# Layer-0 gates of batch 0 computed head by head, own staging tiles for batch 0's keys and queries, and the last step's key-wise sums placed ahead of its outputs

## What is computed

```python
xn = _layernorm(x)
x = x + attn(xn) + ffn(xn)      # both read xn
# attn: 16 heads of 8 features, softmax attention over keys and values shared by all heads
#       q = (xn Wq^T + bq) * 8**-0.5 ;  k, v = split(xn Wkv^T + bkv)
# ffn ("SwitchHead"): 8 heads, 8 experts each, and per head a full 1024 x 1024 attention
def _get_sel_gate(x, w, route_scale):
    raw = einsum('bsd,ed->bse', x, w).reshape(B, S, H, E)        # 8 heads x 8 experts
    vals, idx = top_k(sigmoid(raw), 2)
    vals = vals / clip(vals.sum(-1, keepdims=True), 1e-09) * route_scale
    return (one_hot(idx, E) * vals[..., None]).sum(-2)           # a dense gate
v   = einsum('bshep,bshe->bhsp', xv, gate_v)       # values of a head: 8 experts, gated
att = softmax(einsum('bhqp,bhkp->bhqk', q, k) * SCALE)
out = einsum('bshep,hepd->bsd', ctx * gate_o, o_w)
```

## Time and profile before

| | us |
|---|---|
| median of 3 runs (lowest, highest) | 3180.81 (3178.78, 3181.18) |
| the profiled execution, its own time | 3167.05 |
| its span, from the first to the last instruction | 3165.2 |
| PE busy | 2945.3 (93%) |
| DVE busy | 2427.8 (77%) |
| POOL busy | 1846.8 (58%) |
| ACT busy | 1619.2 (51%) |
| the step loop's first matmul (L293) starts at | 55.16 |
| the last batch's projection (L444) starts at | 2572.41 |

### The profile page before, as it was taken

How to read it: one execution, slowest core, us unless ns; L and a number is a source line. 1 busy time by engine, 2 the same in 40 slices (tenths; PEclk the granted TensorE clock), 3 DMA queues, 4 the chain that set the end, 5 groups by cost and what they waited for, 6 DMA issues and landing times. The chain is left out here.

```text
span 3165.2 us, 51840 instructions
## 1 busy us (share of the span) xinstructions
PE 2945.3 (93%) x17486; PEld 2054.4 (65%) x17486; DVE 2427.8 (77%) x4551; ACT 1619.2 (51%) x3277; POOL 1846.8 (58%) x2277
## 2 busy tenths in 40 slices
PE   4999999999999999999999999999999965798997
PEld 2666666666676666666666666666676643466674
DVE  7788898888889988898898988888888652245343
ACT  1455555555555555555555555555555621444634
POOL 2556666666676666666666676666666535334330
PEclk7999999999999999999999999999999978899998
DMA  5000001100100110101001100010010021133222
GB/s 168 21 22 22 22 22 32 32 22 23 37 27 22 32 32 22 29 23 36 29 22 32 32 22 23 22 43 28 22 39 22 10 43 45 56 89 110 84 76 85
DMA packets 139849, 124.63 MB, mean 39 GB/s; under 512 B 28410, under 2 KB 122116, under 8 KB 139492
## 3 DMA queue, kind: packets, MB, share of 16 engines
q1 hardware_dynamic: 125892, 88.46, 10.0%
q0 software_dynamic: 10160, 30.17, 3.0%
q10 hardware_dynamic: 3536, 2.69, 0.5%
HBM read 97.49 MB, written 29.30 MB: 40 GB/s over the span
## 5 line engine op out<-in xcount | busy, mean ns | idle before, releaser
L849 POOL TENSOR_TENSOR m_vprod<-m_vprod 128x512 f32<-128x512 f32 x256 | 336.1, 1313 | 721.4 <-DVE m_vprod L1223 721.4
L1210 DVE TENSOR_REDUCE m_peaks<-m_ring 128x1 f32<-128x512 f32 x1024 | 643.4, 682 | 23.9 <-PE m_ring L293 22.7
L957 ACT ACTIVATE m_expA<-m_ring 128x512 f32<-128x512 f32 x1024 | 543.9, 605 | 162.4 <-PE m_ring L366 159.2
L928 ACT ACTIVATE m_prob<-m_ring,m_negs 128x512 f32<-128x512 f32 x512 | 347.4, 684 | 404.4 <-DVE m_negs L1261 403.6
L344 PE MATMUL m_ring<-m_probT,m_vs 128*128 128x256 f32 x2048 | 473.8, 384 | 11.7 <-DVE m_oprod L1294 10.2
L344 PEld LDWEIGHTS m_ring<-m_probT,m_vs 128*128 128x128 f32 x2048 | 379.9, 190 | 83.8 <-issue 35.1
L1294 DVE TENSOR_TENSOR m_oprod<-m_ring,m_go 128x512 f32<-128x512 f32 x512 | 347.4, 685 | 73.5 <-POOL k_x L862 44.8
L1223 DVE TENSOR_TENSOR m_vprod<-m_ring,m_gate 128x512 f32<-128x512 f32 x512 | 348.8, 685 | 68.2 <-PE m_ring L99 41.0
L1251 DVE TENSOR_REDUCE m_negs<-m_ring 128x1 f32<-128x512 f32 x512 | 346.0, 685 | 39.2 <-PE m_ring L99 37.0
L858 POOL TENSOR_TENSOR m_oprod<-m_oprod 128x512 f32<-128x512 f32 x256 | 327.9, 1281 | 70.6 <-DVE m_oprod L1294 70.4
L938 ACT ACTIVATE m_probT<-m_ring 128x512 f32<-128x512 f32 x512 | 301.0, 605 | 103.9 <-PE m_ring L332 98.3
(11 more groups left out here) (311 smaller groups left out, 5396.9 us busy)
## 6 DMA issues: line engine op xcount, KB each, us to landing
m_wraw<-in_v_w SPq DMA_DIRECT2D x32, 512.0 KB, 4.0
m_qf<-q_dram SPq DMA_DIRECT2D x128, 128.0 KB, 2.7
m_wraw<-in_o_w SPq DMA_DIRECT2D x32, 512.0 KB, 4.0
q_dram<-m_kf SPq DMA_DIRECT2D x24, 256.0 KB, 3.0
listed<-in_pad SPq DMA_DIRECT2D x6, 897.0 KB, 12.2
m_xg<-listed SPq DMA_DIRECT2D x39, 138.0 KB
m_rows<-answers SPq DMA_DIRECT2D x8, 512.0 KB, 4.0
sums_dram<-m_sumsT ACTq DMA_DIRECT2D x128, 18.0 KB
```

What stands on the lines that cost most here:

```text
L849: vchain(pool.tensor_tensor(vprod[:, 0:512], vprod[:, 0:512], vprod[:, 512:1024], ALU.add))
L928: act.activation(prob[t % 2][:, c * 512:(c + 1) * 512], ring.home["scores", n, t, c][:, :], ACT.Exp, bias=neg[t % 2], accum_out=den[n % 2] ...
L957: act.activation(expA[hh][:, c * 512:(c + 1) * 512], ring.home["scT", n, k, hh, c][:, :], ACT.Exp)\
L1210: v.tensor_reduce(peaks[:, t, hh, c:c + 1], ring.home["peaks", n, t, hh, c][:, :], AX.X, ALU.max)\
```

## The change

It has two parts. The first is at the start:

- batch 0's keys and queries get four staging tiles of their own, cut out of `m_probT` (`first_kf`); ACT doesn't wait any more between the halves, and its first copy into `m_probT` waits for the stores instead;
- PE makes batch 0's keys and queries ahead of its logits, ACT copies them ahead of the exponentials of the gates, and the upper half of x and of the first value weights comes behind these; the square root at the start isn't held by the wait for the constants any more;
- batch 0's gates are computed for one head at a time (`first_gates(h, part)`, over 128x128: 8 token tiles, 2 gates, 8 experts), in staging tiles cut out of `m_oT`. Head 0's 17 parts come ahead of the step loop, head h's in iteration i = h - 3, two parts at each place of `batch_work`, three at place 7.

```diff
+        h_v, h_one, h_c, h_other = (oT[:, k * P:(k + 1) * P].rearrange("p (g e) -> p g e", e=ES) for k in range(4))
+        first_kf = probT[0][:, :, :].rearrange("p t q -> p (t q)").rearrange("p (w q d) -> p w q d", w=2, q=2)
...
+        def kf_of(b, what, q):
+            return kf[:, :] if b else first_kf[:, what, q, :]
...
-                    if b or q:
+                    if b:
                         act.wait_ge(ks_ready, 2 * b + q)
-                        act.wait_ge(q_stored, 64 + (96 * b if b else 48 * q))
+                        act.wait_ge(q_stored, 64 + 96 * b)
...
+                def first_gates(h, part):
+                    if not 0 <= h < HS:
+                        return
+                    flat = gate_of[0][:, :, :].rearrange("p t (k g e) -> p (t k) g e", k=2, e=ES)[:, :, h, :]
+                    if part == 0:
+                        v.wait_ge(gates_exp, 4)
+                    gate_part(gs, part, flat, (h_v, h_one, h_c, h_other, h_m, h_pair, h_inv), 2 * TPB)
+                    if part == 16:
+                        gates_kept(v.tensor_tensor(flat, h_one, h_other, ALU.add))
...
                 def batch_work(i, place):
+                    for part in range(2 * place, 2 * place + 2 + place // 7):
+                        first_gates(i + 3, part)
...
+                lower_keys(0, 0)
+                lower_keys(0, 1)
                 for l in range(4):
                     keep_v32(0, l)
-                lower_keys(0, 0)
                 for part in range(17):
-                    gates(0, part)
-                lower_keys(0, 1)
+                    first_gates(0, part)
                 lower_qk()
-                for part in range(17, 34):
-                    gates(0, part)
                 for i in range(-2, N0 + 3):
+                    if i == N0 - 1:
+                        invert_dens(B - 1)
```

`gate_part` holds the 17 parts as they were, with the tiles as arguments. The second part of the change is at the end: the last step (n = 31) is taken out of the loop on PE and ACT and written out, with all its `scores_by_key`, `exps` and `sum_by_key` moved up between the rest, ACT's store of the sums behind them, and `invert_dens(B - 1)` on DVE ahead of its iteration 31:

```diff
+                keyed(last, 7)
+                outputs(last, 1, 0)
+                outputs(last, 1, 1)
+                turn(last, 4, 1)
+                sum_by_key(last, 7)
+                turn(last, 5, 0)
+                outputs(last, 2, 0)
...
+                key_exps(last, 7)
+                keep_turned(last, 4, 1)
+                keep_sums(last)
+                store_sums(last)
```

More of the change, by code:

```diff
@@ L368, in scores_by_key, with keyed @@
                         .then_inc(scT_made, 1)
+                def keyed(n, k):
+                    for hh in range(2):
+                        for c in range(2):
+                            scores_by_key(n, k, hh, c)
                 def sum_by_key(n, k):
@@ L483, in _ @@
                 turn_xn(0, 1)
-                for l in range(4):
-                    logits(0, l)
                 for q in range(2):
@@ L488, in _ @@
                     queries(0, q)
+                for l in range(4):
+                    logits(0, l)
                 qk_products()
-                for i in range(-2, N0 + 3):
+                for i in range(-2, N0):
                     outputs(i - 2, 7, 1)
@@ L638, in _ @@
                     values(i + 1, 3, 0)
+                last = N0 - 1
+                outputs(last - 1, 7, 1)
+                sum_by_key(last, 2)
+                keyed(last, 3)
+                weigh(last, 0)
+                sum_by_key(last, 3)
+                keyed(last, 4)
+                turn(last, 3, 0)
+                turn(last, 3, 1)
+                outputs(last, 0, 0)
+                outputs(last, 0, 1)
+                sum_by_key(last, 4)
+                keyed(last, 5)
+                scores(last, 4, 0)
+                scores(last, 4, 1)
+                weigh(last, 1)
+                sum_by_key(last, 5)
+                keyed(last, 6)
+                turn(last, 4, 0)
+                scores(last, 5, 0)
+                scores(last, 5, 1)
+                sum_by_key(last, 6)
+                keyed(last, 7)
[5 more added lines that the diff above has]
+                outputs(last, 2, 0)
+                turn(last, 5, 1)
+                scores(last, 6, 0)
+                outputs(last, 2, 1)
+                scores(last, 6, 1)
+                outputs(last, 3, 0)
+                weigh(last, 2)
+                turn(last, 6, 0)
+                scores(last, 7, 0)
+                scores(last, 7, 1)
+                outputs(last, 3, 1)
+                outputs(last, 4, 0)
+                turn(last, 6, 1)
+                outputs(last, 4, 1)
+                turn(last, 7, 0)
+                turn(last, 7, 1)
+                weigh(last, 3)
+                for t in (5, 6, 7):
+                    outputs(last, t, 0)
+                    outputs(last, t, 1)
+                turn_xo(B - 2, 0)
+                turn_xo(B - 2, 1)
                 routing(B - 2)
@@ L668, in store_queries @@
                         rows = slice(2 + part * HD, 2 + (part + 1) * HD)
-                        sp.dma_start(q_dram[b % 2][:, rows, q * 512:(q + 1) * 512], kf[:, :]).then_inc(q_stored, 16)
+                        sp.dma_start(q_dram[b % 2][:, rows, q * 512:(q + 1) * 512], kf_of(b, 1, q)).then_inc(q_stored, 16)
                 def load_queries(n):
@@ L958, in exps, with key_exps @@
                         .then_inc(exps_made, 1)
+                def key_exps(n, k):
+                    for hh in range(2):
+                        for c in range(2):
+                            exps(n, k, hh, c)
                 def keep_sums(n):
@@ L1045, in keep_queries @@
                     act.wait_ge(q_made, 2 * b + q + 1)
-                    act.wait_ge(ks_ready, 2 * (b + 1) if b else q + 1)
-                    if b or q:
+                    if b:
+                        act.wait_ge(ks_ready, 2 * (b + 1))
                         act.wait_ge(q_stored, 64 + 48 * (2 * b + q))
-                    act.activation(kf[:, :], ring.home["queries", b, q][:, :], ACT.Identity, bias=bq[:, :], scale=HD ** -0.5)\
+                    act.activation(kf_of(b, 1, q), ring.home["queries", b, q][:, :], ACT.Identity, bias=bq[:, :], scale=HD ** -0.5)\
                         .then_inc(q_kept, 1)
@@ L1089, in batch_work @@
                         routing_exps(early)
+                roots(1, slice(0, TPB))
                 act.wait_ge(consts_loaded, 16 * n_consts)
-                roots(1, slice(0, TPB))
                 keep_xnT(0, 0)
                 keep_xnT(0, 1)
-                upper_x(0)
-                upper_wv(0, ahead=True)
-                for l in range(4):
-                    sigmoid_exps(0, l)
                 for q in range(2):
@@ L1101, in _ @@
                     keep_queries(0, q)
+                for l in range(4):
+                    sigmoid_exps(0, l)
+                upper_x(0)
+                upper_wv(0, ahead=True)
                 keep_qk()
-                for i in range(-2, N0 + 3):
+                for i in range(-2, N0 - 1):
                     softmax(i, 2, 1)
@@ L1381, in gates @@
-                    if part == 6:
-                        gs(v.scalar_tensor_tensor(out=g_v[:, :, :], in0=g_one[:, :, :], scalar=3.0e38, in1=g_v[:, :, :],
-                                                  op0=ALU.mult, op1=ALU.add))
-                    if part == 7:
-                        gs(v.tensor_reduce(g_pair[:, 1, :], g_v[:, :, :], AX.X, ALU.min))
-                    if part == 8:
-                        gs(v.tensor_tensor(g_c[:, :, :], g_v[:, :, :], spread(g_pair[:, 1, :], ES), ALU.is_equal))
@@ L1679, in _ @@
                     gate_outputs(i + 1, 3, 1)
-                invert_dens(B - 1)
                 keep_routing(B - 2)
```

128 lines of the change are left out of this document (93 added, 35 removed).

## The result

The changed kernel took 3195.85 us (median of 5 runs, 3190.92 to 3203.52) against 3178.78 us of the kernel before in the same comparison (5 runs, 3165.74 to 3181.18): ratio 1.0071, 95% interval 1.0053 to 1.0089. (The quotient of the two medians is smaller, 1.0054; all ratios in this text are those of the timed comparison.) The forecast was 3160.8 us, the range 3151 to 3178. The profiled execution of the changed kernel took 3190.92 us with a span of 3189.1; that of before 3167.05 with 3165.2.

A forecast was written before the change was run, and what follows sets the result against it. PE was taken to bound the steps, with DVE close behind and its gates holding the start. Start -22.5, steps +10 and end -7.5 make -20 us: 3180.8 to 3160.8 us, range 3151 to 3178.

The forecast's parts named there:

- The start: Ahead of the step loop: PE's first matmul 22.5 us sooner, ends 18 and 23.5.
- The price in the steps: Step loop: moved gates cost 9 us of DVE a head and lengthen the steps by 10 us, ends 3 and 24.
- the two ends I had put: Steps' price: 3 us if gates nearly all fill idle time, 24 us if 4 us idle stay at 9 us a head.
- The rival "slower": Steps: POOL-DVE lock makes each two-input operation wait 0.6 us, 14.2 us a head, 51 us price, 3202 us; chance 0.07.
- The lock: Steps: DVE instructions with two SBUF inputs and GpSimd instructions reading SBUF lock each other out for a whole instruction.
- The decision point: Steps: the rival "slower" decides from a price of 30 us on, about 11 us for a head.
- The end: Layer 0's last outputs to its projection: PE starts the projection sooner, 7.5 us gained, ends 4 and 10.

The follow-up runs named there:

- `e_no_later`: The changed kernel with the gates of heads 1 to 7 of batch 0 left out; ratio to the kernel before 0.9919.
- The doses: The kernel before with DVE work added in every second iteration from 8 to 28: reductions lengthened 23 stretches by 64.4 us, two-input operations by 104.9 (traces only).
- `e_places`: The changed kernel with each later head's gate operations unchanged but moved to places 3, 4 and 6; ratio to the kernel before 1.0027.
- `e_reduce`: The changed kernel with nine 128x128 two-input operations of each of heads 1 to 7 replaced by reductions at the same places; ratio to the kernel before 1.0009.

## Why the prediction was wrong

- **The start** was right in kind and 3 us too large: 19.45 us for PE's entry, and 20.0 us where nothing is added behind it (`e_no_later`), in the range of 18 to 23.5. Both of its ways were later than I had them. The queries landed at 33.6, not 29.8, since the stores took 5.94 us instead of 3.6 and began a microsecond later. DVE was ready for the split at 32.7, not 30.4: head 0's gates began 1.7 us sooner than I had put, but took 10.6 us instead of 6.4, since I had charged nothing for POOL's start-up work beside them.
- **The price in the steps** is the step that failed: "the end where DVE's overrun is its busy time plus 1 us of idle time that stays, against the old length", 10 us, measured 51. DVE's work was sized rightly, 9 us a head against 9.1 measured (63.7 / 7), though not the way I had it: a few parts were held by up to 1.1 us each, not all by 0.2. What was wrong is that 7 to 9 us of its idle time would be used. The idle time stayed, 6.2 to 9.2 us in a stretch. These are short waits for products and sums of others, spread through the step. My reading of them is that work put in front of an instruction delays what PE and ACT need next, PE stops, and DVE then waits for PE. The waits bear it out: PE's grew from 2.4 to 17.7 us, 13.9 of them for DVE, and DVE's for PE from 11.8 to 15.7. Neither of the two ends I had put (3 and 24 us, with 4 us idle that stay) held it.
- I had drawn the slack from two stretches: 7 us more DVE (62.4 to 69.6) cost PE 0.2 us. That work is the next batch's gates, and it stands there in both. The doses show that more behind it is paid for: a stretch with 63.4 us of DVE became 5.2 us longer for 6.1 us of work put at one place. What makes the two differ (what stands beside the other batch's parts, or the order of PE's work around them) these runs don't settle.
- **The rival "slower"** had the figure, 51 us and 3202, and its mechanism in part. That it had the figure is luck. It took 14.2 us a head with 3 us idle that stay; measured were 9.1 us with 6 to 9, and the two errors cancel. The lock makes 16 to 20 of the 51 us (`e_places`, `e_reduce`), the amount of work 31 to 35. The decision point, 30 us, was about right: with 31 and 35 us the kernels are at 1.0009 and 1.0027.
- **What of it is PE's clock**: in the five long stretches PE's busy time grew by 20 us of the 41, at granted clocks of 0.92 to 1.00 against 0.96 to 1.00. One minus the granted clock, times the length, gives 3.4 us lost before and 16.4 now, so by this estimate the clock makes 13 of the 20; the other 7, 1.8 of them in a stretch at full clock, stay open. The clock fell in the stretches in which PE's idle time had grown, in the doses' too (0.98 and 0.94, PE busy 2.1 and 3.3 us more), but not in the fifth, where PE was idle for 5.5 us. No run held the clock up with the same waits, so how long the steps would be at full clock stays open.
- **The end** was right as a sum: 7.5 predicted, 7.9 in the trace, 7.3 timed. Within it two errors cancel, which is luck: `keep_routing` came 3.2 us sooner, not 1.3, and DVE's chain from there to the projection took 10.05 us, not 8.1, since POOL's work held its choice. PE idles 10.6 us before the projection, against 8 to 10 predicted.

## What to carry to other kernels

In a loop in which two engines hand work to each other all the time, don't take the idle time of the second for slack: charge added work at its full length unless a run shows otherwise. Here a microsecond of DVE cost 0.8 to 1.2 us, what PE's clock took included. Cutting one wide operation into eight small ones multiplies its cost on DVE (28 us for the two halves of the kernel before, hand-over included, against 46 us for eight heads at best and 74 us in the changed kernel, without it), and putting the gates off paid here only where they stayed wide. Where it must stand in a loop, put two-input operations where GpSimd isn't released by the instruction in front of them; here that alone was worth 16 us (`e_places`).

## What the runs showed that I had not expected

- A DVE instruction with two SBUF inputs that started just behind one of GpSimd's was done only 0.1 to 0.6 us after the other, whatever its own size: 128x128 parts of 0.28 us took 1.27 to 1.37 us (L1505, L1516), a 128x512 one at the start 2.71, one over 128x64 at the end 1.00.
- One-input scalings from SBUF to SBUF do the same (1.29 us against 0.21), reductions of the same input don't (at most 0.29 in all runs).
- Where it happens is fixed by the program: L1505's seven durations lie within 33 ns of each other and L1516's within 11 ns.
